# One tile of every ninth gather section fetched by the sync engine; group transfers issued by ScalarE

## The chip, the cores and the metric

The kernel runs on one core of one Trainium2 chip. The metric is the device time of one execution in microseconds, the median of several runs. A core has five engines with queues of their own: PE (TensorE, matrix products), DVE (VectorE), ACT (ScalarE), POOL (GpSimd) and SP (the sync engine, which computes nothing and issues transfers). Transfers run on 16 DMA engines. Engines meet only at semaphores.

## The reference, cut to what matters

A graph layer and a feed-forward layer over 12,500 nodes of 256 numbers each; 212,500 edges, sorted by destination.

```python
def layer(x, src, dst, edge_weight):
    xn = _layernorm(x)
    msgs = xn[src] * edge_weight[:, None]          # 212,500 rows of 256
    agg = segment_sum(msgs, dst, num_segments=12500)
    x = x + agg @ W.T + b
    H = gelu(_layernorm(x) @ W1 + b1)               # 1024 wide
    probs = softmax(H @ Wg + bg)                    # 8 experts
    e = argmax(probs)
    return x + probs[e] * (H @ Wd[e] + bd[e])
```

What concerns this change is `xn[src]`: row numbers held in memory say which rows of a table have to be fetched.

## The kernel before, in words

**Normalised table.** First all nodes are normalised and written to a table in DRAM, `xn_table` (12,800 rows of 1 KB). That is done at some 77 us.

**Gather steps.** The edges are cut into tiles of 128, one edge per partition, and the tiles into 104 sections of 16 (`NG`, `STEP_TILES`), 1,664 tiles in all. A ring in the on-chip memory, `xring`, holds three sections (`SECTIONS`). It is a part of the tensor `big`, so that the trace names it `big`. POOL fills it: `gather_section` (L398) issues one indirect DMA per tile (L403), which takes 128 row numbers from a column of `src_i` and fetches 128 rows of 1 KB. POOL's program is unrolled over all sections. Before tiles 0 and 8 of a section it waits (L402) until TensorE has read the section that held the same ring slot, three sections earlier. TensorE's `gather_step` (L505) waits for the 16 tiles of its section (L507; there is a semaphore for each ring slot, `s_gath[h]`), multiplies them with narrow selection matrices into `psR` (L515, 32 matmuls, whose end sets the slot free through `s_edge_mm`), and places the partial sums (L527), which DVE adds up.

**Group steps.** The nodes are in 25 groups of 512 (`NF`). When all edges into a group are summed, a group step stands between gather steps, in an order worked out on the chip (`steps_i`): messages, residual, layer norm, first layer, gate and the choice of an expert. TensorE's part is `hidden` (L582), `messages` and `transpose_xn2`; ACT's part is `copy_xn2T` (L458) and `hidden` (L463), with `gate_parts` (L469) at its end; DVE's part is `normalize` and `second_part` (L1018), which copies the transposed hidden rows into `rows` (L1025) after a wait on `s_rows_free` (L1020).

**SP's queue.** After the loads of the start, SP issues the three transfers of each group: `store_x2` (L351, the residual rows to `row_table`), `load_x` (L356, the next group's `x`) and `store_rows` (L361, hidden rows and logits to `row_table`). SP waits for each store to land (L353, L363); after the second it raises `s_rows_free` (L364). After the last gather steps it loads the experts' weights (`Wd`, L379) and biases (L381).

**Routed stage.** At the end 105 tiles of nodes, sorted by expert, run through POOL's indirect loads of `row_table` rows (L420), eight transposes (L648), eight matmuls with the expert's weights (L658), and an indirect store (L428). POOL begins when the node lists are there (`s_perm`) and all rows are stored (`s_rows_free`).

Of the kernel before, what the change touches and what calls it, by code (L numbers as in the profile page):

```python
# [15 lines left out]
F32 = mybir.dt.float32  # L16
I32 = mybir.dt.int32
# [2 lines left out]
AX = mybir.AxisListType  # L20
DVE = mybir.EngineType.DVE
PE = mybir.EngineType.PE

P = 128
N = 12500
C = 256
# [6 lines left out]
GROUP = 512  # L33
QB = GROUP // P
NF = -(-N // GROUP)
# [3 lines left out]
STEP_TILES = 16  # L39
NG = -(-EDGES // (P * STEP_TILES))  # L40
SECTIONS = 3
# [5 lines left out]
HALF_LANES = LANES // 2  # L47
TILES = NG * STEP_TILES
TABLE = TILES + STEP_TILES
STEPS = NG + NF  # L50

SLOT = GROUP + P
# [2 lines left out]
NS = 1 << (2 + -(-STEP_TILES * P // GROUP) - 1).bit_length()  # L55
ACC0 = STEP_TILES
MM0 = SECTIONS * STEP_TILES
GATE_COLS = LANES
ROW = C + HID + E
LOGITS = C + HID  # L60
# [30 lines left out]
        self.eng.wait_ge(self.sem, self.base + self.n)  # L91


def build(nc, x, srcT, dstT, wT, gnn_WT, gnn_b, W1, b1T, Wg, bg, Wd, bd, out):
    assert PAD_ROW + P <= NODES and NB % LN_ROWS == 0
    ctx = ExitStack()
    with ctx:
        def sb(name, shape, dt=F32):
            return ctx.enter_context(nc.sbuf_tensor(name, shape, dt))
# [4 lines left out]
        def sem(name):  # L104
            return ctx.enter_context(nc.semaphore(name))

        xn_dram = nc.dram_tensor("xn_table", (NODES, C), F32, kind="Internal").ap()
        row_dram = nc.dram_tensor("row_table", (NODES, ROW), F32, kind="Internal").ap()


# [3 lines left out]
        xring = big[:, 0:SECTIONS * STEP_TILES * C].rearrange("p (t c) -> p t c", c=C)  # L114
# [8 lines left out]
        xg, xn2 = (big[:, after_wd + a * QB * C:after_wd + (a + 1) * QB * C].rearrange("p (q c) -> p q c", c=C)  # L123
                   for a in range(2))
# [39 lines left out]
        rows = sb("rows", [P, QB, ROW])  # L164
# [44 lines left out]
        tile0, owner, empty, node = (small[:, 2 * P + a * P:2 * P + a * P + NT] for a in range(4))  # L209
# [28 lines left out]
        s_pass = sem("pool_waits_passed")  # L238
        s_pass_dve = sem("dve_waits_passed")
        s_gath = [sem(f"gathered{h}") for h in range(SECTIONS)]  # L240
        s_sel = sem("sel_ready")
        s_edge_mm = sem("edge_matmul_done")
        s_narrow_eq = sem("narrow_onehots")
# [8 lines left out]
        s_xg = sem("xg_loaded")  # L252
        s_x2_st = sem("x2_stored")
        s_lg = sem("logits_ready")
        s_xn2 = sem("xn2_ready")
# [9 lines left out]
        s_rows = sem("rows_ready")  # L265
        s_rows_free = sem("rows_free")
        s_rows_st = sem("rows_stored")
# [28 lines left out]
        ybuf = [xg[:, i, :] for i in range(RING2)]  # L296
        tbuf = [xn2[:, i, :] for i in range(RING2)]
        st_in = stage[:, 0, 0:RING2]
        st_out = sb("st_out", [P, RING2], I32)
        negmax = sb("negmax", [P, RING2])  # L300
        expv = sb("expv", [P, RING2, E])
# [12 lines left out]
        def load_columns(ap, engine, top):  # L314
            return nc.values_load_multi_w_load_instructions(
                ap, engines=(engine,), min_val=0, max_val=top,
                skip_runtime_bounds_check_because="columns and kinds are worked out within their bounds")[1]
# [3 lines left out]
        @block.sync  # L321
        def _(sp):
            xr = x.rearrange("(p r) c -> p r c", p=P)
            for c in range(LN_CHUNKS):
                sp.dma_start(ln_rows[:, c * LN_ROWS:(c + 1) * LN_ROWS, :],
                             xr[:, c * LN_ROWS:(c + 1) * LN_ROWS, :]).then_inc(s_ln_load[c], 16)
            sp.dma_start(src_i[:, :], srcT[:, :]).then_inc(s_src, 16)
            sp.dma_start(dst_i, dstT[:, :]).then_inc(s_edges, 16)
            sp.dma_start(base_i, dstT[0, :].partition_broadcast(P)).then_inc(s_edges, 16)
            xnr = xn_dram.rearrange("(p r) c -> p r c", p=P)  # L330
            for c in range(LN_CHUNKS):

                sp.wait_ge(s_ln_applied, (c + 1) * LN_ROWS)
                sp.dma_start(xnr[:, c * LN_ROWS:(c + 1) * LN_ROWS, :],
                             ln_rows[:, c * LN_ROWS:(c + 1) * LN_ROWS, :]).then_inc(s_xn_stored, 16)
            sp.dma_start(w_f[:, :], wT[:, :]).then_inc(s_weights, 16)
            sp.dma_start(wt[:, :, :], gnn_WT.rearrange("(k p) o -> p k o", p=P)).then_inc(s_weights, 16)
            sp.dma_start(w1[:, :, :], W1.rearrange("(k p) h -> p k h", p=P)).then_inc(s_weights, 16)
            sp.dma_start(wg[:, :, :], Wg.rearrange("(c p) e -> p c e", p=P)).then_inc(s_weights, 16)
            sp.dma_start(b1[:, :], b1T[:, :]).then_inc(s_weights, 16)  # L340
            sp.dma_start(gnn_b_bc[:, :], gnn_b.partition_broadcast(P)).then_inc(s_weights, 16)
            sp.dma_start(bg_bc[:, :], bg.partition_broadcast(P)).then_inc(s_weights, 16)

            sp.sem_inc(s_rows_free, 1)
            sp.wait_ge(s_xn_stored, 16 * LN_CHUNKS)
            sp.dma_start(xg[:, :, :], x[0:GROUP, :].rearrange("(q p) c -> p q c", p=P)).then_inc(s_xg, 16)

            def store_x2(f):

                sp.wait_ge(s_xn2, f + 1)  # L350
                sp.dma_start(row_dram[bass.ds(f * GROUP, GROUP), 0:C].rearrange("(q p) c -> p q c", p=P),  # L351
                             xg[:, :, :]).then_inc(s_x2_st, 16)
                sp.wait_ge(s_x2_st, f * 16 + 16)  # L353

            def load_x(f):
                sp.dma_start(xg[:, :, :], x[bass.ds(f * GROUP, GROUP), :]  # L356
                             .rearrange("(q p) c -> p q c", p=P)).then_inc(s_xg, 16)

            def store_rows(f):
                sp.wait_ge(s_rows, f + 1)  # L360
                sp.dma_start(row_dram[bass.ds(f * GROUP, GROUP), C:ROW].rearrange("(q p) c -> p q c", p=P),  # L361
                             rows[:, :, C:ROW]).then_inc(s_rows_st, 16)
                sp.wait_ge(s_rows_st, f * 16 + 16)  # L363
                sp.sem_inc(s_rows_free, 1)  # L364

            store_x2(0)
            load_x(1)
            with sp.Fori(0, NF - 2) as f:
                store_x2(f + 1)
                load_x(f + 2)  # L370
                store_rows(f)
            store_x2(NF - 1)
            store_rows(NF - 2)


            sp.wait_ge(s_edge_mm, TILES + MM0)
            sp.wait_ge(s_ffn, (NF - 1) * FFN_LINKS + 2)
            for e in range(E):
                sp.dma_start(wd[:, e * HC:(e + 1) * HC, :],  # L379
                             Wd[e].rearrange("(c p) o -> p c o", p=P)).then_inc(s_wd, 16)  # L380
            sp.dma_start(bd_bc, bd.rearrange("e c -> (e c)").partition_broadcast(P)).then_inc(s_bd, 16)  # L381
            store_rows(NF - 1)

        @block.gpsimd
        def _(pool):
# [11 lines left out]
            pool.wait_ge(s_xn_stored, 16 * LN_CHUNKS)  # L397
            def gather_section(g):  # L398
                h = g % SECTIONS
                for j in range(STEP_TILES):  # L400
                    if j % (STEP_TILES // 2) == 0:
                        pool.wait_ge(s_edge_mm, g * STEP_TILES + STEP_TILES // 2 + j)  # L402
                    nc.gpsimd.indirect_dma_start(  # L403
                        out=xring[:, h * STEP_TILES + j, :], out_offset=None, in_=xn_dram[:, :],
                        in_offset=bass.IndirectOffsetOnAxis(
                            ap=src_i[:, g * STEP_TILES + j:g * STEP_TILES + j + 1], axis=0)
                    ).then_inc(s_gath[h], 16)
# [40 lines left out]
        def _(act):  # L448
# [9 lines left out]
            def copy_xn2T(f):  # L458
                for k in range(KC):
                    act.wait_ge(s_xt, f * KC + k + 1)  # L460
                    nc.scalar.activation(xn2T[:, k, :], psH[k][:, :], ACT.Identity).then_inc(s_xtc, 1)

            def hidden(f):  # L463
                for c in range(HC):
                    act.wait_ge(s_h, f * HC + c + 1)
                    nc.scalar.activation(hidT[:, c, :], psH[c % 2][:, :], ACT.Gelu,  # L466
                                         bias=b1[:, c:c + 1]).then_inc(s_gelu, 1)
                act.wait_ge(s_gp, f + 1)
                nc.scalar.activation(gate_parts[:, :], psG[:, :], ACT.Identity).then_inc(s_gc, 1)  # L469

            copy_xn2T(0)
            with act.Fori(0, NF - 1) as f:
                hidden(f)
                copy_xn2T(f + 1)
            hidden(NF - 1)


            def routed_act(t, i):
                for k in range(2):
# [15 lines left out]
        def _(pe):  # L495
# [8 lines left out]
            pe.wait_ge(s_tabs, 1)  # L504
            def gather_step(g, h):  # L505

                pe.wait_ge(s_gath[h], (g + (SECTIONS - h)) * STEP_TILES * 16 // SECTIONS)  # L507
                wide, = load_columns(octs_i[0:1, bass.ds(g, 1), 0:1].rearrange("a b c -> a (b c)"), PE, 1)
                with pe.If(wide == 0):
                    pe.wait_ge(s_narrow, g + 1)  # L510
                    for o in range(OCTS):
                        for odd in range(2):
                            for j in range(OCT // 2):
                                t = h * STEP_TILES + o * OCT + 2 * j + odd
# [662 lines left out]
```

## Time and profile before

| | |
|---|---|
| time, median of 3 runs | 2781.99 us (2778.76 to 2784.24) |
| the profiled execution's own time | 2780.53 us |
| its span, from the first to the last instruction | 2778.4 us |
| busy share of the span | PE 68%, POOL 66%, DVE 39%, ACT 16% |
| mean granted TensorE clock | 0.851 |
| DMA queues' share of the 16 engines | POOL's 36.7%, SP's 11.7% |
| the stretch of the gathers | 76.88 us to 2194.07 us |

Busy time counts computing instructions and POOL's indirect DMAs, for which POOL works out the addresses; SP's issues, register work and waits are not in it. A share of the whole span mixes three stages: the table (to 77 us), the gather and group steps (to some 2290 us) and the routed stage. For each, the question is which engine the others wait for.

### The profile page before, as it was taken

How to read it: one execution, taken by the hardware profiler on the slowest of the kernel's cores; microseconds unless marked ns; L12 is line 12 of the kernel's file. 1: busy time of each engine (PE TensorE's matmuls, PEld its weight loads, DVE VectorE, ACT ScalarE, POOL GpSimd, SP SyncE). 2: the span in 40 equal slices, each digit the busy share in tenths (PEclk: the TensorE clock that was granted, in tenths of full speed). 3: DMA queues.
4: the chain of work that ended last, by engine and by line, in shares of the span. 5: the costliest groups of instructions: out<-in, count | busy, mean ns of one | idle time of the engine just before them, and what ended most of it. 6: DMA issues, size and time to landing. Idle time of an engine off the chain costs nothing.

```text
span 2778.4 us, 39308 instructions
## 1 busy us (share of the span) xinstructions
PE 1877.3 (68%) x10522; PEld 1192.6 (43%) x10523; DVE 1079.9 (39%) x3491; ACT 444.4 (16%) x847; POOL 1842.4 (66%) x1988
## 2 busy tenths in 40 slices
PE   0235675666756667666667566675667777999998
PEld 0122343333433333333334233343333446888887
DVE  8522443334433344343444234443344453333332
ACT  7000110100101001010011000110001113333332
POOL 0677777777777777777777777777777403555553
PEclk9966887888878789788888788887888888999999
DMA  9434444444444444444444344443444354555554
GB/s 396 150 103 119 149 148 120 134 148 147 149 117 132 149 149 148 119 135 147 148 149 149 104 148 149 148 149 111 141 149 149 108 204 152 182 181 179 182 179 128
DMA packets 153598, 420.31 MB, mean 151 GB/s; under 512 B 33320, under 2 KB 67499, under 8 KB 150880
## 3 DMA queue, kind: packets, MB, share of 16 engines
q0 software_dynamic: 100032, 300.27, 36.7%
q1 hardware_dynamic: 53536, 119.73, 11.7%
q14 instruction: 23, 0.19, 0.0%
q8 instruction: 7, 0.11, 0.0%
HBM read 328.02 MB, written 92.82 MB: 151 GB/s over the span
## 4 chain that ended last, share of the span: by engine, by line
POOL 45%; PE 27%; issue 18%; DVE 5%; DMA 2%; DVEq 1%; SPq 0%; POOLq 0%
POOL big L403 45%; PE psA L658 3%; PE psH L658 3%; PE psG L658 3%; PE psE L658 3%; PE psH L592 2%; PE psR L515 2%; PE psA L614 1%; PE psG L600 1%; PE psA L569 1%; DMA src_i<-in_srcT 1%; PE psH L648 1%; PE psE L521 1%; PE psA L648 1%; PE psE L648 1%
## 5 line engine op out<-in xcount | busy, mean ns | idle before, releaser
L403 POOL DMA_INDIRECT big<-xn_table,src_i x1664 | 1610.6, 968 | 581.5 <-issue 579.3
L515 PE MATMUL psR<-big,sel_narrow 128*32 128x256 f32 x3328 | 297.6, 519 | 597.7 <-DMA big<-xn_table,src_i 409.8
L515 PEld LDWEIGHTS psR<-big,sel_narrow 128*32 128x32 f32 x3328 | 127.1, 141 | 715.0 <-issue 630.6
L466 ACT ACTIVATE hidT<-psH,b 128x512 f32<-128x512 f32 x200 | 137.4, 687 | 1506.5 <-PE psH L592 1506.5
L592 PE MATMUL psH<-xn2T,w 128*128 128x512 f32 x800 | 374.4, 624 | 0.0
L900 DVE COPY parts<-psR 128x512 f32<-128x512 f32 x104 | 71.5, 687 | 439.0 <-PE psR L515 438.9
L521 PE MATMUL psE<-w,ident 128*128 128x512 f32 x416 | 240.8, 707 | 0.0
L592 PEld LDWEIGHTS psH<-xn2T,w 128*128 128x128 f32 x800 | 157.8, 200 | 182.6 <-issue 181.3
L894 DVE TENSOR_TENSOR place<-iota,shift_f 128x160 f32<-128x160 f32 x104 | 34.5, 332 | 328.8 <-issue 328.8
L420 POOL DMA_INDIRECT rows<-row_table,stage x105 | 104.1, 991 | 86.8 <-POOL stage L417 86.8
L417 POOL COPY stage<-rel_f 128x1 int32 (+1 forms) x105 | 19.2, 183 | 213.4 <-DVEq L1098 107.2
L1025 DVE COPY rows<-psA 128x512 f32<-128x512 f32 x200 | 128.9, 686 | 40.5 <-PE psA L614 35.9
L527 PEld LDWEIGHTS psE<-place,parts 128*128 128x128 f32 x832 | 107.7, 191 | 84.1 <-DVE parts L900 51.4
L521 PEld LDWEIGHTS psE<-w,ident 128*128 128x128 f32 x416 | 87.0, 234 | 131.8 <-issue 131.8
L890 DVE TENSOR_TENSOR big<-psE,big 128x160 f32 x208 | 67.5, 325 | 185.0 <-PE psE L527 170.2
L428 POOL DMA_INDIRECT out<-big,st_out x105 | 107.3, 1022 | 43.6 <-issue 30.4
L614 PE MATMUL psA<-ident,hidT 128*128 128x128 f32 x800 | 122.6, 287 | 18.4 <-DVE rows L1025 18.4
L527 PE MATMUL psE<-place,parts 128*128 128x80 f32 x832 | 107.1, 272 | 27.6 <-DVE parts L900 27.6
L614 PEld LDWEIGHTS psA<-ident,hidT 128*128 128x128 f32 x800 | 85.3, 142 | 86.9 <-DVE rows L1025 49.7
L560 PE MATMUL psE<-col_oh,big 128*128 128x40 f32 x208 | 38.6, 347 | 95.2 <-DVE big L961 95.2
L658 PE MATMUL psA<-big,hidT 128*128 x432 | 98.7, 382 | 0.0
L569 PE MATMUL psA<-wt,aggs 128*128 128x256 f32 x400 | 92.8, 386 | 6.6 <-DVE aggs L930 6.6
(207 smaller groups left out, 2415.2 us busy)
## 6 DMA issues: line engine op xcount, KB each, us to landing
row_table<-rows SPq DMA_DIRECT2D x25, 2064.0 KB, 8.0
big<-xn_table,src_i POOLq DMA_INDIRECT x1664
big<-in_x SPq DMA_DIRECT2D x10, 1280.0 KB, 17.4
xn_table<-big SPq DMA_DIRECT2D x10, 1280.0 KB, 13.2
big<-in_x SPq DMA_DIRECT2D x25, 512.0 KB
row_table<-big SPq DMA_DIRECT2D x25, 512.0 KB, 3.9
big<-in_Wd SPq DMA_DIRECT2D x8, 1024.0 KB, 12.7
hidT<-in_dstT SPq DMA_DIRECT2D x2, 840.0 KB, 30.5
```

Source lines behind the costliest of these rows:

```text
L403: nc.gpsimd.indirect_dma_start(out=xring[:, h * STEP_TILES + j, :], out_offset=None, in_=xn_dram[:, :], in_offset=bass.IndirectOffsetOnAxi ...
L420: nc.gpsimd.indirect_dma_start(out=grow[i], out_offset=None, in_=row_dram[:, :], in_offset=bass.IndirectOffsetOnAxis(ap=st_in[:, i:i + 1], ...
L428: nc.gpsimd.indirect_dma_start(out=out[:, :], out_offset=bass.IndirectOffsetOnAxis(ap=st_out[:, i:i + 1], axis=0), in_=ybuf[i], in_offset= ...
L466: nc.scalar.activation(hidT[:, c, :], psH[c % 2][:, :], ACT.Gelu, bias=b1[:, c:c + 1]).then_inc(s_gelu, 1)
L515: mm = nc.tensor.matmul(psQ[j * LANES:(j + 1) * LANES, o * C:(o + 1) * C], sel_narrow[:, t, :], xring[:, t, :], start=(odd == 0), stop=(od ...
L521: nc.tensor.matmul(psW[:, :], ident[:, :], w1[:, 0, 0:512], start=True, stop=True)
L527: mm = nc.tensor.matmul(psW[:, at:at + SPAN], parts[:, o, k * P:(k + 1) * P], place[:, o, :], start=True, stop=True)
L569: mm = nc.tensor.matmul(psA[q // 2][:, (q % 2) * C:(q % 2 + 1) * C], aggs[:, k, q * P:(q + 1) * P], wt[:, k, :], start=(k == 0), stop=(k = ...
L592: mm = nc.tensor.matmul(psH[c % 2][:, :], w1[:, k, c * P:(c + 1) * P], xn2T[:, k, :], start=(k == 0), stop=(k == KC - 1))
L614: mm = nc.tensor.transpose(psA[i % 2][:, j * P:(j + 1) * P], hidT[:, 4 * half + j, q * P:(q + 1) * P], ident[:, :])
L658: mm = nc.tensor.matmul(psY2[i], hT2[i][:, c, :], wd[:, bass.ds(e8 + c, 1), :], start=(c == 0), stop=(c == HC - 1))
L1025: nc.vector.tensor_copy(rows[:, q, C + half * 512:C + (half + 1) * 512], psA[i % 2][:, :]).then_inc(s_ev, 1)
```

## The change

Of every ninth section, from section 6 on (6, 15, ..., 96: `ROW_TILES` = 11 sections, all in ring slot 0), POOL leaves out the last tile. SP fetches it: it loads the 128 row numbers, reads eight at a time into registers, copies each row by a DMA of its own from `xn_table` to a second table in DRAM (`row_tiles`), waits until all have landed and the ring slot is free, and loads the tile into the ring by one DMA. TensorE's wait for slot 0 counts the missing tiles out by register arithmetic, and waits for SP's tile count as well. The group transfers go from SP's queue to ACT's.

```diff
+CYCLE = 9
+ROW_SECTION = 6
+ROW_TILES = -(-(NG - ROW_SECTION) // CYCLE)
+ROWS_AT_ONCE = 8
+ROW_SLOT_FREE = (ROW_SECTION + 1) * STEP_TILES
...
         @block.sync
...
-            sp.sem_inc(s_rows_free, 1)
             sp.wait_ge(s_xn_stored, 16 * LN_CHUNKS)
             sp.dma_start(xg[:, :, :], x[0:GROUP, :].rearrange("(q p) c -> p q c", p=P)).then_inc(s_xg, 16)
...
-            store_x2(0)
-            load_x(1)
-            with sp.Fori(0, NF - 2) as f:
-                store_x2(f + 1)
-                load_x(f + 2)
-                store_rows(f)
-            store_x2(NF - 1)
-            store_rows(NF - 2)
+            sp.sem_inc(s_row_tile, 1)
+            with sp.Fori(0, ROW_TILES) as t:
+                sp.dma_start(row_src[0:1, :], srcR[bass.ds(t * (CYCLE * STEP_TILES) + ROW_SECTION * STEP_TILES + STEP_TILES - 1, 1), :]
+                             ).then_inc(s_row_src, 16)
+                sp.wait_ge(s_row_src, t * 16 + 16)
+                sp.sem_inc(s_pass_sp, 1)
+                with sp.Fori(0, P // ROWS_AT_ONCE) as p8:
+                    node = load_columns(row_src[0:1, bass.ds(p8 * ROWS_AT_ONCE, ROWS_AT_ONCE)], SP, N - 1)
+                    for a in range(ROWS_AT_ONCE):
+                        sp.dma_start(tile_dram[bass.ds(t * P + p8 * ROWS_AT_ONCE + a, 1), :],
+                                     xn_dram[bass.ds(node[a], 1), :]).then_inc(s_row[a], 16)
+                for a in range(ROWS_AT_ONCE):
+                    sp.wait_ge(s_row[a], t * (16 * P // ROWS_AT_ONCE) + 16 * P // ROWS_AT_ONCE)
+                sp.sem_inc(s_pass_sp, 1)
+                sp.wait_ge(s_edge_mm, t * (CYCLE * STEP_TILES) + ROW_SLOT_FREE)
+                sp.sem_inc(s_pass_sp, 1)
+                sp.dma_start(xring[:, STEP_TILES - 1, :], tile_dram[bass.ds(t * P, P), :]).then_inc(s_row_tile, 16)
 
             sp.wait_ge(s_edge_mm, TILES + MM0)
...
             sp.dma_start(bd_bc, bd.rearrange("e c -> (e c)").partition_broadcast(P)).then_inc(s_bd, 16)
-            store_rows(NF - 1)
...
             def gather_section(g):
                 h = g % SECTIONS
-                for j in range(STEP_TILES):
+                for j in range(STEP_TILES - (g % CYCLE == ROW_SECTION)):
...
         @block.scalar
...
+            def store_x2(f):
+
+                act.wait_ge(s_xn2, f + 1)
+                act.dma_start(row_dram[bass.ds(f * GROUP, GROUP), 0:C].rearrange("(q p) c -> p q c", p=P),
+                              xg[:, :, :]).then_inc(s_x2_st, 16)
+
+            def load_x(f):
+                act.wait_ge(s_x2_st, f * 16)
+                act.dma_start(xg[:, :, :], x[bass.ds(f * GROUP, GROUP), :]
+                              .rearrange("(q p) c -> p q c", p=P)).then_inc(s_xg, 16)
+
+            def store_rows(f):
+                act.wait_ge(s_rows, f + 1)
+                act.dma_start(row_dram[bass.ds(f * GROUP, GROUP), C:ROW].rearrange("(q p) c -> p q c", p=P),
+                              rows[:, :, C:ROW]).then_inc(s_rows_st, 16)
+
+            def free_rows(stored):
+                act.wait_ge(s_rows_st, stored * 16)
+                act.sem_inc(s_rows_free, 1)
...
+            with act.Fori(1, NF - 2) as f:
                 hidden(f)
+                free_rows(f)
+                store_x2(f + 1)
                 copy_xn2T(f + 1)
+                load_x(f + 2)
+                store_rows(f)
+            hidden(NF - 2)
+            free_rows(NF - 2)
+            store_x2(NF - 1)
+            copy_xn2T(NF - 1)
+            store_rows(NF - 2)
             hidden(NF - 1)
+            free_rows(NF - 1)
+            store_rows(NF - 1)
+            free_rows(NF)
+            act.wait_ge(s_x2_st, NF * 16)
...
         @block.tensor
             def gather_step(g, h):
-                pe.wait_ge(s_gath[h], (g + (SECTIONS - h)) * STEP_TILES * 16 // SECTIONS)
+                if h == 0:
+                    nth = (g + SECTIONS) // SECTIONS
+                    pe.wait_ge(s_gath[h], (nth * (CYCLE // SECTIONS * STEP_TILES - 1) + 2) // (CYCLE // SECTIONS) * 16)
+                    pe.wait_ge(s_row_tile, nth // (CYCLE // SECTIONS) * 16 + 1)
+                else:
+                    pe.wait_ge(s_gath[h], (g + (SECTIONS - h)) * STEP_TILES * 16 // SECTIONS)
```

The new input `srcR` is `srcT` with a tile's 128 row numbers side by side in memory.

## Rows read from the trace of the kernel before

**Rows 1.** Groups by line on POOL: count, busy us and mean ns, idle before.

```profile
L403 POOL DMA_INDIRECT big<-xn_table,src_i x1664 | 1610.6, 968 | 581.5 <-issue 579.3 <-PE psR L515 2.1
```

**Rows 2.** Waits by engine: us in total, times, longest us.

```profile
POOL big L403 <- issue: 579.3, 1657, 74.9
POOL big L403 <- PE psR L515: 2.1, 7, 0.3
...
PE psR L515 <- DMA big<-xn_table,src_i: 409.8, 32, 15.6
```

**Rows 3.** POOL in order of time: the first gather and the last one.

```profile
76.88 1.16 POOL L403 DMA_INDIRECT big<-xn_table,src_i  x1 [74.90 <-issue]
...
2193.12 0.95 POOL L403 DMA_INDIRECT big<-xn_table,src_i  x1 [0.30 <-issue]
```

**Rows 4.** PE and POOL in order of time: where the ring was tightest (section 16).

```profile
393.89 1.93 PE L515 MATMUL psR<-big,sel_narrow 128*32 128x256 f32 x32 [1.79 <-issue]
...
403.41 0.94 POOL L403 DMA_INDIRECT big<-xn_table,src_i  x1 [0.30 <-issue]
```

**Rows 5.** PE in order of time: section 101.

```profile
2155.59 3.64 PE L515 MATMUL psR<-big,sel_narrow 128*32 128x256 f32 x32 [11.17 <-DMA big<-xn_table,src_i]
```

**Rows 6.** SP's issues, DVE's eight-value load: ns min/median/max, first and last start.

```profile
L351 SPq DMA_DIRECT2D row_table<-big x25: 372/372/396, 211.4 to 2237.3; - x25
L351 SPq FUSED_REGOPS  x23: 55/55/67, 291.3 to 2183.6; - x23
L351 SPq MOVE row_table<-big x23: 29/29/29, 291.4 to 2183.7; - x23
...
L315 DVEq TENSOR_LOAD <-full_i x26: 596/611/623, 296.5 to 2289.4; - x26
...
L379 SPq DMA_DIRECT2D big<-in_Wd x8: 385/2923/4464, 2258.3 to 2274.5; - x8
```

**Rows 7.** DMA issues: count, KB each, median us from issue to landing.

```profile
row_table<-big SPq DMA_DIRECT2D x25, 512.0 KB, 3.9
...
b<-in_b1T SPq DMA_DIRECT2D x1, 4.0 KB, 8.0
```

**Rows 8.** SP, POOL and PE in order of time: the first section with a moved tile.

```profile
74.39 3.46 SPq L340 DMA_DIRECT2D b<-in_b1T  x1
...
78.93 0.38 SPq L346 DMA_DIRECT2D big<-in_x  x1
...
162.25 3.64 PE L515 MATMUL psR<-big,sel_narrow 128*32 128x256 f32 x32 [13.73 <-DMA big<-xn_table,src_i]
...
223.18 2.38 PE L515 MATMUL psR<-big,sel_narrow 128*32 128x256 f32 x32 [2.29 <-DVE sel_narrow L857]
```

**Rows 9.** ACT and DVE in order of time: around the hand-over of `rows`.

```profile
306.64 1.09 ACT L461 ACTIVATE xn2T<-psH 128x512 f32<-128x512 f32 x2 [6.15 <-PE psH L578]
...
2191.30 0.60 ACT L469 ACTIVATE big<-psG 128x512 f32<-128x512 f32 x1 [7.77 <-PE psG L600]
...
2191.85 1.29 DVE L1025 COPY rows<-psA 128x512 f32<-128x512 f32 x2 [0.92 <-PE psA L614]
```

**Rows 10.** The end of the groups, SP and POOL, with SP's last release of rows.

```profile
2258.26 19.20 SPq L379 DMA_DIRECT2D big<-in_Wd  x8
...
L364 SPq EVENT_SEMAPHORE  x25: 17/17/17, 314.7 to 2294.2; - x25
...
2301.30 0.18 POOL L417 COPY stage<-rel_f 128x1 int32<-128x1 int32 x1 [107.23 <-DVEq L1098]
```

**Rows 11.** L403 in two stretches: us, POOL busy (count), PE clock, DMA share, GB/s.

```profile
77.00:84.00 7.00, 5.78 (x5) 1.00 1.06 342
306.00:314.00 8.00, 6.17 (x7) 1.00 0.87 321
```

**Rows 12.** POOL and DVE in order of time: a long gather, with SP issuing nothing.

```profile
276.14 1.34 POOL L403 DMA_INDIRECT big<-xn_table,src_i  x1 [0.30 <-issue]
...
275.96 0.69 DVE L929 COPY aggs<-big 128x1024 f32 x1 [3.64 <-issue]
```

More of the change, by code:

```diff
@@ L22 @@
 PE = mybir.EngineType.PE
+SP = mybir.EngineType.SP
 P = 128
@@ L91, in __call__, with build @@
         self.eng.wait_ge(self.sem, self.base + self.n)
-def build(nc, x, srcT, dstT, wT, gnn_WT, gnn_b, W1, b1T, Wg, bg, Wd, bd, out):
+def build(nc, x, srcT, srcR, dstT, wT, gnn_WT, gnn_b, W1, b1T, Wg, bg, Wd, bd, out):
     assert PAD_ROW + P <= NODES and NB % LN_ROWS == 0
@@ L107, in build @@
         xn_dram = nc.dram_tensor("xn_table", (NODES, C), F32, kind="Internal").ap()
+        tile_dram = nc.dram_tensor("row_tiles", (ROW_TILES * P, C), F32, kind="Internal").ap()
         row_dram = nc.dram_tensor("row_table", (NODES, ROW), F32, kind="Internal").ap()
@@ L240, in build @@
         s_gath = [sem(f"gathered{h}") for h in range(SECTIONS)]
+        s_row_src = sem("row_sources_loaded")
+        s_pass_sp = sem("sp_waits_passed")
+        s_row = [sem(f"rows_landed{a}") for a in range(ROWS_AT_ONCE)]
+        s_row_tile = sem("row_tile_ready")
         s_sel = sem("sel_ready")
@@ L298, in build @@
         st_in = stage[:, 0, 0:RING2]
+        row_src = sb("row_src", [1, P], I32)
         st_out = sb("st_out", [P, RING2], I32)
@@ L342, in _ @@
             sp.dma_start(bg_bc[:, :], bg.partition_broadcast(P)).then_inc(s_weights, 16)
-            sp.sem_inc(s_rows_free, 1)
             sp.wait_ge(s_xn_stored, 16 * LN_CHUNKS)
             sp.dma_start(xg[:, :, :], x[0:GROUP, :].rearrange("(q p) c -> p q c", p=P)).then_inc(s_xg, 16)
[L348 to L364, printed above, removed]
@@ L469, in hidden @@
                 nc.scalar.activation(gate_parts[:, :], psG[:, :], ACT.Identity).then_inc(s_gc, 1)
-            copy_xn2T(0)
-            with act.Fori(0, NF - 1) as f:
+            def store_x2(f):
[13 more added lines that the diff above has]
+                act.sem_inc(s_rows_free, 1)
+            act.sem_inc(s_rows_free, 1)
+            store_x2(0)
+            copy_xn2T(0)
+            load_x(1)
+            hidden(0)
+            store_x2(1)
+            copy_xn2T(1)
+            load_x(2)
+            store_rows(0)
+            with act.Fori(1, NF - 2) as f:
                 hidden(f)
+                free_rows(f)
+                store_x2(f + 1)
                 copy_xn2T(f + 1)
+                load_x(f + 2)
[5 more added lines that the diff above has]
+            store_rows(NF - 2)
             hidden(NF - 1)
+            free_rows(NF - 1)
+            store_rows(NF - 1)
+            free_rows(NF)
+            act.wait_ge(s_x2_st, NF * 16)
             def routed_act(t, i):
@@ L1156 @@
         "srcT": edges("src", 0),
+        "srcR": np.ascontiguousarray(edges("src", 0).T),
         "dstT": edges("dst", N - 1),
```

## The prediction

> **What bounds the kernel now.** Start with the groups by line: the costliest is POOL's indirect DMA, 1,664 of 968 ns, with 581.5 us of idle time ahead of them, almost all "issue", time in which nothing was waited for [rows 1]. That suggests an engine that works without pause. The list of waits settles it: POOL's "issue" time is 579.3 us in 1,657 pieces, the longest of them the 74.9 us before the first gather; only 7 gaps, 2.1 us together, end with something of TensorE's, and none is longer than 0.3 us [rows 2]. In order of time every gather, the plain ones too, has a gap of 0.30 us ahead of it [rows 3, 4], so those seven are the ordinary gap, in which a semaphore happened to arrive. Nobody holds POOL up. From 76.88 us to 2193.12 + 0.95 = 2194.07 us [rows 3] it issues 1,664 gathers: 2117.2 / 1664 = 1.272 us each (1.25 us for a plain one, the rest being longer ones). TensorE is the one who waits: 409.8 us for gathered tiles [rows 2].
>
> Two checks are needed before "one gather less" may be read as "1.27 us less". **Does the ring let POOL run ahead?** I compared the start of each section on POOL with the end of the products that free its slot. The tightest of the 101 sections is 16: products end at 393.89 + 1.93 = 395.82, POOL wants the slot at 403.41 [rows 4], so 7.6 us are spare. POOL reaches such a point at most one gather earlier relative to TensorE (one tile in nine sections), and 6.3 us remain. **Does the end hang on POOL?** The chain of waits passes from POOL to TensorE for good at section 101: TensorE has been idle for 11.17 us when its tiles land [rows 5]. All that comes later (two more sections, the last groups, the routed stage) hangs on that moment, and all eleven lightened sections (6 to 96) lie ahead of it.
>
> **The change part by part.**
>
> *Removed:* 11 gathers on POOL, 11 x 1.272 = **14.0 us** (11 x 1.25 = 13.75 at the plain price).
>
> *Added on SP:* 128 copies per tile, 1,408 in all. The trace has no single-row copy, so I build one from SP's own rows. An issue takes 0.372 us, though it describes 512 KB; address work is one fused register operation of 0.055 and one move of 0.029 for an address [rows 6]. Two addresses: 0.372 + 2 x 0.084 = 0.54. Reading eight numbers into registers took DVE 0.611 us [rows 6], 0.076 per row. Loop branches included, 0.64 us for a copy, 82 us for a tile. Bounds: below, the bare issue, 0.372 (48 us); above, an issue on a queue that is full, as the loads of `Wd` show, median 2.923 (374 us) [rows 6]. I take 0.64, because the group stores, with 512 pieces each, did not fill the queue. Around the copies: the load of the row numbers, at most 8.0 us (the slowest small load of the start), and the landing of the last copies, some 4 us (3.9 for a group's store) [rows 7].
>
> Is that early enough? The first tile is the tightest. SP is free at 78.93 + 0.38 = 79.3; 79.3 + 8 + 82 + 4 = 173; section 3, whose slot is wanted, was read at 162.25 + 3.64 = 165.9; half an issue and 4 us later, at about 178, the tile is in the ring, and TensorE wants it at 223.18 [rows 8]. Spare: 45 us. Later tiles have a cycle of nine sections, 143 x 1.272 = 182 us, against 82 + 12 = 94. The copies are **costed at nothing**, covered by SP's idle time; that cover is gone at (182 - 12) / 128 = 1.33 us per copy.
>
> *Moved to ACT:* three issues a group of about 0.46 us each. `free_rows` and `store_x2` follow `gate_parts`; ACT then waits 6.15 us for its next work [rows 9]. `load_x` and `store_rows` come behind `copy_xn2T`, whose semaphore TensorE already has; ACT is not wanted again until the next group step. `load_x` waits for a store issued some 6 us earlier, longer than its 3.9 [rows 7]. The one new dependence is `s_rows_free`: DVE began copying rows at 2191.85, and `gate_parts`, now ahead of the release on ACT's queue, ended at 2191.90 [rows 9]. Price between nothing (the release may pass on the queue before the activation ends) and some 0.3 us; I take 0.15. It counts only behind section 101, and there only in the first of three steps: in the other two DVE is the later one anyhow. In the other group steps the 6.3 us of ring cover it.
>
> *Moved past SP's queue:* SP no longer waits for group 23's rows before it issues `Wd` (2258.26 before), nor does the last store stand behind it (landed at 2294.2). Both can be earlier, yet POOL's routed stage started only at 2301.30, released by DVE's queue [rows 10]. Worth nothing.
>
> *TensorE's register arithmetic* for slot 0: at section 102, the only such one behind 101, DVE is late with its own register loads, so a few tenths of a us are covered.
>
> **Sum:** 14.0 - 0.15 = 13.85 us. The profiled execution took 2780.53 (span 2778.4), 1.5 below the median; off it that is 2766.7, and off the median of 2781.99 it is **2768.1 us**.
>
> **What speaks against it.** With the copies, POOL's gathers share the DMA engines with 1,408 small transfers. The rows show what heavy company did: between 306 and 314 us a group's 2 MB store ran, the engines were busy for 0.87 at 321 GB/s, and seven gathers took 6.17 us, 0.88 each inside the window, so plain ones. Between 77 and 84 us, at 342 GB/s, gathers were slower: 5 took 5.78 [rows 11]. But a gather of 1.34 us also stands at 276.14, where SP issues nothing and DVE copies 1,024 columns in SBUF from 275.96 on [rows 12]. So a long gather needs no traffic, and traffic need not make one long; the slow stretch at the start stays unexplained, and is what the second rival below lives on. The Trainium skill, page "DMA: Bandwidth & Descriptors", section "Issuing engines are not separate DMA queues", says that transfers of all issuing engines run on the same 16 DMA engines and interleave; by that rule gathers could land later, though it names no cost on POOL's issue, and the stretch at 306 us shows none.
>
> **The rivals.**
> 1. *The copies can't be overlapped* (slower). Each waits in a full queue for the earlier ones. For it: no trace of before has small DRAM-to-DRAM transfers in flight. Against: the load of `b1`, issued at 74.39, took 8.0 us to land, and meanwhile SP issued others, the last at 78.93 [rows 7, 8]. It decides from 1.33 us a copy. At the full queue's 2.923, a cycle is 374 + 12 = 386; the eleventh tile is ready at 79 + 11 x 386 = 4325; section 96 wants it at 76.9 + 97 x 16 x 1.272 - 14 = 2037, so the time would be 2768 + 2288, about 5050 us. The Trainium skill, same page, section "Rules for kernel authors", says that transfers under 64 KB are mostly overhead and should be joined, and section "Anatomy of one DMA" gives a transfer of GpSimd's path a fixed cost of 2.0 us; if that did not overlap, the estimate from that page would be 128 x 2.0 + 12 = 268 us a cycle, and some 3760 us in all. No run here shows it for such copies.
> 2. *The copies slow POOL's issue* (slower). SP copies for 11 x 82 = 902 us, during which 709 gathers are issued. It decides from 14.0 / 709 = 20 ns each. Were they 1.02 us instead of 0.95, the time would be 2782 + 50 - 14 = 2818; at the 1.41 of the first four, 3090. Against it: [rows 11, 12].
> 3. *The gain is given back in part* (no change). A milder form of the second, 12 to 20 ns a gather, or group steps stretched by more than the spare 6.3 us: 2777 to 2787 us.
>
> **How the numbers follow.** Forecast 0.82, first rival 0.06, second 0.06, third 0.06. A measurement of this kernel can tell about 0.2%, 5.6 us. Hence faster 0.82, same 0.06, slower 0.12. The forecast's own range: the runs of before spread from 2778.8 to 2784.2; minus 14.0 and minus 13.4 gives 2764.8 to 2770.8. To take in a mild slowing of the gathers I go up to 2776.
>
> **What would show it.** Right: 1,653 gathers at L403 with the mean near 968 ns and the last one ending near 2180; the waits of POOL still "issue" alone; 1,408 issues on SP near 0.4 us, a tile's 128 within some 82 us; SP then waiting for the slot; TensorE never ending a wait on a row tile; ACT's hidden work as before. Wrong: TensorE's waits in slot 0 ended by SP's tile (first rival), a mean of L403 above 988 ns (second), gaps of POOL longer than 0.3 us that end with `psR` (third).

## The result and the profile after

The changed kernel takes 2771.09 us (median of 12 runs, 2764.61 to 2777.01), the kernel before in the same sessions 2784.64 us (12 runs, 2778.76 to 2789.0): a ratio of **0.9948, 95% interval 0.9937 to 0.9959**. The two medians lie 13.6 us apart; the ratio, which rests on all the runs, stands for 14.5 us less (11 to 18). Forecast was 13.85 us less.

The profiled execution has a span of 2762.9 us. Its page has POOL's group, with a new line number, as the answer to [rows 1]; the waits of POOL and of TensorE answer to [rows 2].

```profile
L405 POOL DMA_INDIRECT big<-xn_table,src_i x1653 | 1600.2, 968 | 578.6 <-issue 574.9 <-PE psR L563 3.7
```

```profile
POOL big L405 <- issue: 574.9, 1641, 75.0
POOL big L405 <- PE psR L563: 3.7, 12, 0.3
...
PE psR L563 <- DMA big<-xn_table,src_i: 379.6, 32, 13.9
```

Eleven instructions fewer, the same mean, and still no gap of POOL that a wait has made longer than 0.3 us. TensorE ends no wait on SP's tile (`row_tiles` does not occur among what it waited for). So POOL set the pace as before. Where the time went is seen in order of time at two points, POOL's last gather and TensorE's section 101:

```profile
2179.81 0.95 POOL L405 DMA_INDIRECT big<-xn_table,src_i  x1 [0.30 <-issue]
```

```profile
2142.27 3.64 PE L563 MATMUL psR<-big,sel_narrow 128*32 128x256 f32 x32 [11.32 <-DMA big<-xn_table,src_i]
```

The last gather ends at 2180.76 instead of 2194.07 [rows 3], 13.3 us earlier; section 101 begins at 2142.27 instead of 2155.59 [rows 5], also 13.3, after nearly the same idle time (11.32 us, before 11.17). One pair of executions tells this to some 4 us only: section 101 begins between 2153.5 and 2157.6 us in the three profiled executions with 1,664 gathers, and between 2139.1 and 2143.0 in the five with 1,653. What lies behind (2762.9 - 2142.3 = 620.6 us, before 622.8) differs by 2 us; over the profiled executions of all kernels here except the one that was 3.7% slower, twelve in all, this tail lies between 620.6 and 627.4 us without following the edits, so these 2 us are no more than the spread between executions.

SP's new work, by its tile and in order of time (ns min/median/max; start, us):

```profile
L369 SPq MOVE row_tiles<-xn_table x2816: 29/29/63, 86.2 to 1928.7; - x188
L369 SPq DMA_DIRECT2D row_tiles<-xn_table x1408: 501/521/1780, 86.3 to 1928.9; - x176
...
DMA to landing us min/median/max: 2.0/2.2/7.7
```

```profile
210.62 0.38 SPq L376 DMA_DIRECT2D big<-row_tiles  x1
211.57 0.30 SPq L362 DMA_DIRECT2D row_src<-in_srcR  x1
214.74 123.33 SPq L369 DMA_DIRECT2D row_tiles<-xn_table  x128
347.79 0.36 SPq L376 DMA_DIRECT2D big<-row_tiles  x1
```

A tile's 128 copies take 123.33 us, 0.964 each, not the 0.64 I had built. The issue alone is 0.521. Still, SP is idle for long: it waits 460.4 us in ten waits for a free ring slot:

```profile
SPq L375 <- PE psR L563: 460.4, 10, 67.7
SPq L365 <- DMA row_src<-in_srcR: 27.4, 11, 6.5
SPq L372 <- DMA row_tiles<-xn_table: 14.6, 21, 2.1
```

### The profile page after: what moved, and what is told of

Same layout as the page of the kernel before. It is cut to its first block, busy times and chain, and to the rows that moved or that the text cites. A ratio compares the mean times of both kernels' runs of the same rounds, so it can differ in the third digit from the quotient of the medians.

```text
span 2762.9 us, 45766 instructions
## 1 busy us (share of the span) xinstructions
PE 1879.3 (68%) x10522; PEld 1189.4 (43%) x10523; DVE 1081.3 (39%) x3491; ACT 415.2 (15%) x824; POOL 1832.5 (66%) x1977
## 3 DMA queue, kind: packets, MB, share of 16 engines
q1 hardware_dynamic: 61126, 44.18, 5.0%
## 4 chain that ended last, share of the span: by engine, by line
POOL 45%; PE 28%; issue 18%; DVE 5%; DMA 2%; DVEq 1%; SPq 0%; POOLq 0%
POOL big L405 45%; PE psA L706 3%; PE psH L706 3%; PE psG L706 3%; PE psE L706 3%; PE psH L640 3%; PE psR L563 2%; PE psA L617 1%; PE psA L662 1%; DMA src_i<-in_srcT 1%; PE psG L648 1%; DMA big<-xn_table,src_i 1%; PE psH L696 1%; PE psE L569 1%; PE psA L696 1%
## 5 line engine op out<-in xcount | busy, mean ns | idle before, releaser
L563 PEld LDWEIGHTS psR<-big,sel_narrow 128*32 128x32 f32 x3328 | 127.5, 142 | 698.7 <-issue 633.7
L419 POOL COPY stage<-rel_f 128x1 int32 (+1 forms) x105 | 19.3, 184 | 211.0 <-DVEq L1146 106.3
L942 DVE TENSOR_TENSOR place<-iota,shift_f 128x160 f32<-128x160 f32 x104 | 34.2, 329 | 314.8 <-issue 314.8
L575 PEld LDWEIGHTS psE<-place,parts 128*128 128x128 f32 x832 | 107.2, 191 | 86.4 <-DVE parts L948 56.7
```

What stands on the lines that cost most here:

```text
L563: mm = nc.tensor.matmul(psQ[j * LANES:(j + 1) * LANES, o * C:(o + 1) * C], sel_narrow[:, t, :], xring[:, t, :], start=(odd == 0), stop=(od ...
L575: mm = nc.tensor.matmul(psW[:, at:at + SPAN], parts[:, o, k * P:(k + 1) * P], place[:, o, :], start=True, stop=True)
```

## The experiments

Four parts of the change could have paid or cost: eleven gathers less, the copies beside POOL, the transfers on ScalarE, and SP's time. The first three runs take the first three singly; the later ones bear on SP's time and on the price of a gather. Each edit is shown against the changed kernel, cut to what matters, unless the text says otherwise.

### Only the group transfers on ScalarE

```diff
-            with sp.Fori(0, ROW_TILES) as t:
...
-                for j in range(STEP_TILES - (g % CYCLE == ROW_SECTION)):
+                for j in range(STEP_TILES):
...
```

> ScalarE issues the group transfers as in the changed kernel, but POOL gathers all 1,664 tiles and SP copies none. Theory (the gain is eleven gathers of 1.272 us on POOL, and everything else lies beside it): no change, within 3 us of the kernel before (ratio 0.999 to 1.001), the last gather still ends near 2194 us, the mean gather stays near 968 ns. Rival (the moved transfers, and with them the earlier load of Wd, pay a part of the 14.5 us): faster by 1.5 us or more, out of the stretch behind the last gather. Second rival (the new place of rows_free on ScalarE's queue costs): slower by 0.3 to 3 us, also behind the last gather.

Measured: 2782.99 us against 2782.1 us, ratio 1.0002 (0.9992 to 1.0012); mean gather 969 ns. The move pays nothing and costs nothing that can be measured. The interval reaches from 2 us less to 3 us more; an effect smaller than that stays open. Both rivals would have had to show behind the last gather. In the one profiled execution the tail from section 101 on is 627.4 us, the longest of the twelve; the other ten of these with the transfers on ScalarE have 620.6 to 626.4, so no cost can be read from it.

The changed kernel's trace shows why the release of `rows` costs nothing. In order of time, the group step of [rows 9], just behind section 101: ACT, its queue, and DVE. Below, by its line, the semaphore step of `free_rows`, 25 in all:

```profile
2177.98 0.60 ACT L471 ACTIVATE big<-psG 128x512 f32<-128x512 f32 x1 [7.78 <-PE psG L648]
2178.36 0.38 ACTq L476 DMA_DIRECT2D row_table<-big  x1
2178.52 1.29 DVE L1073 COPY rows<-psA 128x512 f32<-128x512 f32 x2 [0.91 <-PE psA L662]
```

```profile
L491 ACTq EVENT_SEMAPHORE  x25: 17/17/17, 381.8 to 2273.0; - x25
```

`store_x2` stands behind `free_rows` on ACT's queue, and its issue begins 0.38 us after the activation began, 0.22 before it ends: the queue had passed `free_rows` while the activation still ran. (The first of these semaphore steps, at 381.8 us, comes some 0.1 us after its group's activation began, at 381.71.) DVE starts copying 0.54 us after the activation's start, released by TensorE; before it was 0.55 us [rows 9].

### The copies beside all 1,664 gathers, and the lightened sections without copies

```diff
-                sp.dma_start(xring[:, STEP_TILES - 1, :], tile_dram[bass.ds(t * P, P), :]).then_inc(s_row_tile, 16)
...
-                for j in range(STEP_TILES - (g % CYCLE == ROW_SECTION)):
+                for j in range(STEP_TILES):
...
```

> As the changed kernel, but POOL gathers all 1,664 tiles and the copied rows are not loaded into the ring: the 1,408 copies run for nothing. Theory (copies cost POOL nothing): as the kernel before, ratio 0.999 to 1.001, mean gather 967 to 969 ns, last gather ends near 2194 us. Rival (copies slow the gathers issued beside them): each ns on the mean gather is 1.66 us; a mean of 975 ns would be 11 us slower (ratio 1.004), and a part of the gain of the changed kernel would have been given back.

```diff
-                with sp.Fori(0, P // ROWS_AT_ONCE) as p8:
...
-                sp.dma_start(xring[:, STEP_TILES - 1, :], tile_dram[bass.ds(t * P, P), :]).then_inc(s_row_tile, 16)
+                sp.dma_start(xring[:, STEP_TILES - 1, :], xn_dram[bass.ds(t * P, P), :]).then_inc(s_row_tile, 16)
```

> As the changed kernel, but SP makes no copies: it loads eleven tiles from the first 1,408 rows of xn_table, so those tiles hold other rows than the edges name. POOL issues 1,653 gathers. Theory (copies cost nothing): as the changed kernel, 14 us faster than before (ratio 0.9945 to 0.9955), last gather ends near 2180.8 us. Rival (copies cost something): faster than the changed kernel, by the same amount by which the copies alone slow the kernel before, so below 0.994.

Measured: the copies alone 2782.91 us, ratio 1.0001 (0.999 to 1.0012); the lightened sections without copies 2766.54 us, ratio 0.9946 (0.9931 to 0.9961), as the changed kernel. POOL's group in the first and in the second:

```profile
L404 POOL DMA_INDIRECT big<-xn_table,src_i x1664 | 1608.3, 967 | 581.8 <-issue 579.6 <-PE psR L556 2.1
```

```profile
L397 POOL DMA_INDIRECT big<-xn_table,src_i x1653 | 1598.1, 967 | 578.3 <-issue 574.9 <-PE psR L555 3.4
```

967 ns with 1,408 copies beside, 967 without: the second rival needed 20 ns more on the gathers issued beside copies. The first of these traces shows it from within as well: its gathers of at most 1.00 us take 945.6 ns on average while a tile's copies are being issued, and 945.6 while none are. The load on the DMA engines is small. SP's hardware queue in the changed kernel, and in the one without copies (packets, MB, share of 16 engines):

```profile
q1 hardware_dynamic: 61126, 44.18, 5.0%
```

```profile
q1 hardware_dynamic: 16070, 42.65, 4.0%
```

1,408 copies are 45,056 packets, 32 each, and one hundredth of the engines' time. The Trainium skill, page "DMA: Bandwidth & Descriptors", section "Issuing engines are not separate DMA queues", says that the transfers of all issuers interleave on the same engines. No view here tells the 16 engines apart, so the interleaving is not shown; what is shown is that no slowing of POOL's issue came of it.

### A moved tile in every sixth section

```diff
-CYCLE = 9
+CYCLE = 6
...
-                for j in range(STEP_TILES - (g % CYCLE == ROW_SECTION)):
+                for j in range(STEP_TILES - (g >= ROW_SECTION and g % CYCLE == 0)):
...
-                    pe.wait_ge(s_row_tile, nth // (CYCLE // SECTIONS) * 16 + 1)
+                    pe.wait_ge(s_row_tile, g // CYCLE * 16 + 1)
```

> As the changed kernel with a moved tile in every sixth section (6, 12, ..., 102): 17 tiles. POOL loses 17 x 1.272 = 21.6 us. But SP needs 129.2 us for a tile (in the changed kernel: 3.2 for the row numbers, 123.3 for 128 copies, some 1.7 until the last landed, 0.95 for the load), and six sections last 95 x 1.272 = 120.8 us. Theory (SP's time is hidden only while it is shorter than the cycle): the last tile lands at 79.7 + 17 x 129.2 + 2.2 = 2278 us, TensorE begins section 102 there instead of at 2199.6, and the time is 2278 + 579 + 2 = about 2860 us, 2.7% slower than before (2840 to 2880). Rival (SP's copies overlap with its waits further than that, so that the gain goes on): 21 us faster.

Measured: 2888.63 us, ratio 1.0373 (1.0352 to 1.0393): slower, as the theory said, but 28 us later than worked out and above its range (2840 to 2880). Waits, of TensorE and of POOL:

```profile
PE psR L563 <- DMA big<-row_tiles: 322.5, 13, 43.4
PE psR L563 <- DMA big<-xn_table,src_i: 178.5, 18, 15.2
...
POOL big L405 <- PE psR L563: 127.7, 16, 23.6
```

Here is what the forecast's first rival looks like: TensorE waits 13 times for SP's tile, and POOL, for the first time in this study, waits for TensorE. Among SP's own waits there is none for a free slot any more. In order of time, from the first tile's end to the last one's:

```profile
210.94 0.30 SPq L362 DMA_DIRECT2D row_src<-in_srcR  x1
...
2303.43 0.36 SPq L376 DMA_DIRECT2D big<-row_tiles  x1
```

That is 16 tiles in 2303.8 - 210.9 = 2092.9 us, 130.8 each instead of 129.2; 17 x 1.6 = 27 of the 28 us of the miss. The cover ends where the sum put it: 130.8 us do not fit into 120.8.

### Fifteen tiles in every section

Left out here is the last tile of all 104 sections; no copies are made, and TensorE multiplies what the slot held. The edit is shown against the run with the transfers on ScalarE alone:

```diff
-                for j in range(STEP_TILES):
+                for j in range(STEP_TILES - 1):
...
-                pe.wait_ge(s_gath[h], (g + (SECTIONS - h)) * STEP_TILES * 16 // SECTIONS)
+                pe.wait_ge(s_gath[h], (g + (SECTIONS - h)) * (STEP_TILES - 1) * 16 // SECTIONS)
```

> The last tile of all 104 sections is left out and replaced by nothing: TensorE multiplies what the ring's slot held, so the edge sums are those of other data. Group transfers on ScalarE, no copies. POOL issues 1,560 gathers. Theory (POOL alone sets the pace, and the price of a gather holds for many): 102 gathers ahead of the end of section 101, 102 x 1.272 = 130 us faster than before, ratio 0.953, waits of POOL still issue alone. Rival (the ring's spare 7.6 us are eaten three gathers at a time and TensorE, which now waits 410 us for tiles, becomes a second bound): POOL's gaps end with psR for 10 us or more, and the gain is below 120 us (ratio above 0.957).

Measured: 2655.94 us against 2781.41, ratio 0.9547 (0.9526 to 0.9567), 125.5 us less. The theory's 0.953 lies in the interval, the rival's 0.957 and more just outside, and its sign is missing: POOL's gaps that end with `psR` are 2.4 us together, none above 0.3.

```profile
L387 POOL DMA_INDIRECT big<-xn_table,src_i x1560 | 1512.8, 970 | 549.9 <-issue 547.5 <-PE psR L539 2.4
```

So POOL alone sets the pace even with 104 gathers less. The price may have been a little high: section 101 begins at 2029.50, 126.1 us earlier, 126.1 / 102 = 1.236 us a gather. At 1.272 us it would be 129.7, at the plain price of 1.25 us (0.946 busy and 0.30 of gap) 127.5. Since executions with the same number of gathers differ by some 4 us at this point, the trace leans to the plain price and does not exclude the other.

The busy times lean the same way. What a run's gathers are busy beyond 0.946 us each is 1610.6 - 1664 x 0.946 = 36.5 us before, 36.5 in the changed kernel, 37.0 here. If the long gathers became fewer with the gathers, 34.2 would be left here. But the other runs lie between 33.5 and 40.6, and the commonest length itself is between 0.946 and 0.949 us from execution to execution (0.949 in the changed kernel's, by which its 36.5 would be 31.5). That the long gathers do not become fewer is therefore not shown. What the traces show is where they stand: of the 1,577 gathers longer than 1.00 us in all thirteen traces, every one overlaps an instruction of DVE, as in [rows 12], and of the shorter ones about half do (before: 776 of 1,521). DVE has as much work as ever, which would be a reason for them to stay; a removed gather would then be worth a plain one, 1.25 us, and not the mean of 1.272.

### Two moved tiles in fifteen sections

```diff
-CYCLE = 9
+CYCLE = 15
+ODD_AFTER = 6
...
-                for j in range(STEP_TILES - (g % CYCLE == ROW_SECTION)):
+                for j in range(STEP_TILES - (g >= ROW_SECTION and (g - ROW_SECTION) % CYCLE in (0, ODD_AFTER))):
...
+            with sp.Fori(0, ROW_TILES // 2) as pair:
+                for odd in range(2):
+                    row_tile(pair, odd)
```

> As the changed kernel with two moved tiles in every fifteen sections (6, 12, 21, 27, ..., 96, 102): 14 tiles. SP's two tiles take 2 x 130.8 = 262 us by the run with a cycle of six; fifteen sections take 238 x 1.272 = 303 us, so SP keeps up. Section 102 lies behind section 101, from whose landing on TensorE sets the end, so that 13 of the 14 count. Theory (gathers ahead of section 101 are what counts): 13 x 1.272 = 16.5 us faster than before (ratio 0.9941), 2.5 us faster than the changed kernel. Rival (all moved tiles count): 17.8 us (0.9936). Rival (six sections between two moved tiles are too short for SP, TensorE waits for some of the rows): TensorE's waits name the row tile, and the gain is below 14 us.

Measured: 2766.01 us against 2781.41, ratio 0.9942 (0.9927 to 0.9957); 0.9941 was expected. SP keeps up, and TensorE waits for no row tile; 13 and 14 tiles are too near to be told apart, and so is this run from the changed kernel.

### What a copy costs SP

```diff
-                        sp.dma_start(tile_dram[bass.ds(t * P + p8 * ROWS_AT_ONCE + a, 1), :],
-                                     xn_dram[bass.ds(node[a], 1), :]).then_inc(s_row[a], 16)
+                        sp.dma_start(tile_dram[bass.ds(t * P + p8 * ROWS_AT_ONCE + a, 1), :].rearrange("r (h c) -> (r h) c", h=2),
+                                     xn_dram[bass.ds(node[a], 1), :].rearrange("r (h c) -> (r h) c", h=2)).then_inc(s_row[a], 16)
```

> As the changed kernel, each row copied as two pieces of 512 bytes instead of sixteen of 64. Theory (an issue of 0.521 us instead of 0.372 comes from the sixteen pieces spread over sixteen engines): the issue falls to 0.40 us or less, a tile's 128 copies from 123 to about 105 us. Rival (it comes from DRAM addresses in registers on both sides, whatever the pieces): the issue stays at 0.50 to 0.54 us. The time as the changed kernel either way, since SP's time is hidden.

Measured: 2768.24 us in a single run, issue 0.521 us. This decides nothing: the queue shows the same 61,126 packets, so the row still went out in sixteen pieces. The next run removes the other suspect, the second address in a register:

```diff
-                with sp.Fori(0, P // ROWS_AT_ONCE) as p8:
-                    node = load_columns(row_src[0:1, bass.ds(p8 * ROWS_AT_ONCE, ROWS_AT_ONCE)], SP, N - 1)
+                sp.wait_ge(s_row_tile, t * 16 + 1)
+                for p8 in range(P // ROWS_AT_ONCE):
+                    node = load_columns(row_src[0:1, p8 * ROWS_AT_ONCE:(p8 + 1) * ROWS_AT_ONCE], SP, N - 1)
...
-                        sp.dma_start(tile_dram[bass.ds(t * P + p8 * ROWS_AT_ONCE + a, 1), :],
+                        sp.dma_start(tile_dram[p8 * ROWS_AT_ONCE + a:p8 * ROWS_AT_ONCE + a + 1, :],
```

> As the changed kernel, but the 128 copies of a tile are written out and go to 128 rows of DRAM known when the program is built (one table for all tiles; SP waits until the tile before has been loaded), so that only the source address is in a register. In the changed kernel a copy costs SP 0.964 us: an issue of 0.521, register work of 0.064 + 2 x 0.029, and the rest between instructions and in reading row numbers. Theory (the issue of 0.521 instead of 0.372 comes from a second address in registers): the issue falls to 0.36 to 0.40 us, a tile's copies from 123 to about 86 us. Rival (it comes from the copy's going from DRAM to DRAM, or from its sixteen pieces): the issue stays near 0.52, a tile's copies take 100 to 112 us, since one move and some register work still go. The time as the changed kernel either way.

Measured: 2768.63 us in a single run. SP's copies by tile, and in order of time the quickest of the eleven tiles and the middle one:

```profile
L371 SPq DMA_DIRECT2D row_tiles<-xn_table x1408: 492/492/2039, 85.3 to 1910.5; - x176
```

```profile
192.17 96.49 SPq L371 DMA_DIRECT2D row_tiles<-xn_table  x128
...
1279.00 100.33 SPq L371 DMA_DIRECT2D row_tiles<-xn_table  x128
```

The rival holds: a second register address costs the issue 0.03 us, not 0.15. The rest of the step from 0.372 to 0.492 may belong to the path from DRAM to DRAM, to the sixteen pieces or to something else in which the two transfers differ; that was not separated. The shorter issue and the writing out together (no loop, one move and one address sum less) bring a tile's copies from 123.7 us, the median of the changed kernel's eleven tiles, to 100.3, which is 0.78 us a copy.

### The shorter copies in every sixth section, twice

The edits of the run with fixed rows and of the one with a cycle of six together:

```diff
-CYCLE = 9
+CYCLE = 6
...
+                        sp.dma_start(tile_dram[p8 * ROWS_AT_ONCE + a:p8 * ROWS_AT_ONCE + a + 1, :],
```

> The copies to fixed rows, with a moved tile in every sixth section: 17 tiles, 16 of them ahead of section 101. SP's cycle is the copies and some 8 to 10 us around them; six sections last 120.8 us. Theory (SP's time counts only from there on): at 86 to 108 us for the copies the cycle stays hidden, and the gain is 16 x 1.25 = 20 us, ratio 0.9928 to before, 5 to 7 us less than the changed kernel; POOL's waits are issue alone. Rival (SP late as with the loop's copies in every sixth section): TensorE's waits name the row tile, and the time is at or above that of before.

Measured: 2764.18 us against 2779.55, ratio 0.9945 (0.9932 to 0.9959). The cover is back: TensorE's waits name no row tile, POOL's are issue alone, though the sections are the same as in the run that was 3.7% slower. The gain, 15.4 us (11 to 19), is less than the 20 that were expected. To see whether that is the kernel or the occasion, it ran again, beside the changed kernel on the same chip.

> The changed kernel itself, beside the next run on the same chip. Theory (a removed gather is worth the plain 1.25 us, since the 34 to 39 us by which gathers are longer than plain in every run so far do not depend on their number): 11 x 1.25 = 13.75 us faster than before, ratio 0.9951. By the mean price: 14.0 us, too near to tell apart.

> The kernel with copies to fixed rows and a moved tile in every sixth section, beside the changed kernel on the same chip. Theory: 16 moved tiles ahead of section 101 against 11, at 1.25 us each: 6.3 us faster than the changed kernel, 20 us faster than before (ratio 0.9928). Rival (what the first such run showed, 15.4 us, is its true gain: moved tiles beyond the eleventh are worth little, or 2,176 copies cost POOL something): within 2 us of the changed kernel, mean gather 970 ns or more.

Measured, against 2787.36 us before: the changed kernel 2770.56, ratio 0.994 (0.9925 to 0.9954); the seventeen tiles 2766.25, ratio 0.993 (0.9914 to 0.9947). The medians differ by 4.3 us, between the 6.3 of the theory and the 2 of the rival, and the intervals overlap. POOL's groups, of the changed kernel and of the other:

```profile
L405 POOL DMA_INDIRECT big<-xn_table,src_i x1653 | 1597.2, 966 | 578.5 <-issue 576.4 <-PE psR L563 2.1
```

```profile
L407 POOL DMA_INDIRECT big<-xn_table,src_i x1647 | 1598.7, 971 | 576.8 <-issue 573.4 <-PE psR L565 3.4
```

In these two executions the seventeen tiles' gathers were longer by 5 ns, 8 us in all, as the rival said; in the kernel's first run the mean was 970. (The changed kernel's execution was the quickest of its six runs.) It looks like copies that slow POOL, but the traces speak against it. In the seventeen tiles' execution the gathers of at most 1.00 us take 948.4 ns on average while copies are being issued and 948.0 while none are, in the first such run 946.5 and 946.6. The plain length goes with the execution and not with the copies: the commonest is 949 ns here and in the changed kernel's first trace, 946 in its second. That is 3 of the 5 ns, and the rest is within the spread of the long gathers. Whether the moved tiles beyond the eleventh pay in full stays open: 15.4 us the first time, 21.1 the second, against 20. This version is not shown to be faster than the changed kernel.

## Why the prediction was right

**What bounds.** Right: the one view that decided, POOL's idle time with "issue" as its only reason, held in all kernels whose SP kept up, down to 1,560 gathers. The spare time in the ring held as well, also when every section lost a gather.

**Eleven gathers at 1.272 us.** Right. Of the two prices that stood there, the plain one is perhaps the better: the step divided the whole stretch by its gathers, and so gave each a share of the long ones, while the run with 104 fewer gives 1.236 us and points to long ones that stay, without showing it. At 1.25 the term is 13.75, not 14.0 us. On eleven gathers that is less than a measurement shows.

**A copy at 0.64 us.** Mis-sized: 0.964. The step took SP's issue of a store from SBUF, 0.372, for a copy inside DRAM, which takes 0.521 (0.492 with a fixed destination), and allowed nothing between the instructions. Eight copies take 7.71 us, of which issues, moves, address sums and the load of row numbers (0.528 us) are 5.7. The value stayed within its bounds of 0.372 and 2.923, and nothing came of it, because the cover held: the first tile was ready at about 213 us instead of 178, and TensorE began section 6 at 222.74, 10 us later instead of 45. For this tile that was partly luck. By the forecast's own 45 us it would be late from 0.64 + 45 / 128 = 0.99 us a copy on, well below the 1.33 that holds for the later tiles, and 0.964 is only just less.

**Cover gone at 1.33 us a copy.** The figure itself was not measured; that there is such a limit is shown from the other side. With 120.8 us for a tile instead of 182, copies of 0.96 us made the kernel 3.7% slower; with copies at 0.78 the same sections were 0.5 and 0.7% faster than before.

**Transfers on ScalarE, 0.15 us.** Nothing measurable (ratio 1.0002). The trace speaks for the lower bound: the release passes while the activation still runs.

**`Wd` and the last store.** `Wd` was issued at 2210.56 instead of 2258.26, and POOL's routed stage still began when DVE's queue released it, at 2287.04 after a wait of 106.3 us (107.2 before): worth nothing, as said.

**The rivals.** Copies that can't be overlapped: not at this cycle. The Trainium skill, page "DMA: Bandwidth & Descriptors", section "Rules for kernel authors", says that transfers under 64 KB are mostly overhead. The trace agrees, with 0.96 us of SP for 1 KB, but it is an overhead on an engine that had nothing else to do. Copies that slow POOL: not at eleven tiles, by the two runs that put copies and gathers apart, and at seventeen the plain gathers are as long beside copies as without them, within 0.4 ns. A gain given back in part: no gap of POOL that ends with `psR` is longer than 0.3 us, and the time, 2771.09, lies below this rival's 2777 to 2787.

## What to carry to other kernels

When an engine's idle time is all "issue" and the engine behind it waits, an instruction moved off it is worth about its own length, busy time and gap, for as many as the cover allows. If the long instructions come from another engine's work, price it by the plain one and not by the mean; here the two prices lay too near for the runs to decide. For the engine that takes the work over, compare the whole time of one unit, everything around it included, with the time between two units, and do so for the first unit as well, whose time can be shorter. Leave room for a price half as high again as the one you built: here it was 0.964 us against 0.64.

## What was not expected of the hardware

An issue on SP of a 1 KB copy inside DRAM took longer (0.521 us) than that of a 512 KB store from SBUF (0.372 us). A 1 KB row went out as 32 packets, also where the row was written as two pieces of 512 bytes. The Trainium skill, page "DMA: Bandwidth & Descriptors", section "Why a DMA increments its semaphore by 16 and not by 1", says that a transfer is split over up to 16 engines and that each of them ends its share with a write to the semaphore. The trace agrees: the queue has 22,528 packets of 64 bytes for 1,408 copies, 16 each, and as many of 4 bytes more than without copies.

With the group transfers on ScalarE, the table loads ahead of the hidden layer's activations fell from 24 to 1. Before, and in the changed kernel:

```profile
L466 ACT ACT_TABLE_LOAD x24 | 30.8, 1283 | 0.4
```

```profile
L523 ACT ACT_TABLE_LOAD x26 | 33.4, 1283 | 13.8 <-DMA row_table<-rows 13.3
L457 ACT ACT_TABLE_LOAD x2 | 2.6, 1283 | 15.7 <-DVE nmr L776 15.7
L468 ACT ACT_TABLE_LOAD x1 | 1.3, 1283 | 2.1 <-DMA row_table<-big 2.1
```

The 26 loads of the routed stage and the 2 of the table stage are as many as before. The 23 x 1.283 = 29.5 us less (ACT's busy time fell from 444.4 to 415.2) changed nothing in the time that could be measured, as the run with that part alone shows, whose loads are the same as the changed kernel's; ACT waits for TensorE through most of that stretch. The edit also cut the loop over the groups anew; which of the two took the loads away was not separated.
